# First sums and diagonal copies of a fused attention and MLP kernel in another order, and four low parts of W_o on GpSimd

## The chip, the core and the metric

The kernel runs on one core of a Trainium2 chip. The metric is the device time of one execution in microseconds (us), taken as the median of a few executions; lower is better. The engines are TensorE (PE in the profile, PEld its weight loads), VectorE (DVE), ScalarE (ACT), GpSimd (POOL) and SyncE (SP), whose queue issues most of the DMAs. Each works through its own queue in order and waits on semaphores.

## What is computed

The input x is 2 batches of 2048 tokens with 512 features. Four residual blocks follow each other; the change touches the first, and some small preparations of the others that are made beside it:

```python
def modulated_linear(x, s, aff_w, aff_b, w, b):
    style = s @ aff_w.T + aff_b
    w_mod = w[None] * style[:, None, :]
    demod = rsqrt(sum(w_mod * w_mod, axis=2) + 1e-8)
    return einsum('bni,boi->bno', x, w_mod * demod[:, :, None]) + b

kx = modulated_linear(x, s, k_aff_w, k_aff_b, k_w, k_b).reshape(B, N, 16, 32)
A = softmax(einsum('bnhd,bnjd->bnhj', kx, kx) / sqrt(32), axis=-1)
y = modulated_linear(einsum('bnhj,bnjd->bnhd', A, kx), s, o_aff_w, o_aff_b, o_w, o_b)
x = x + y
x = x + low_rank_layer(x)
x = x + modulated_layer_2(x)
x = x + mlp_of_six_normalized_blocks(x)
```

The attention is among the 16 heads of one token. The MLPs of the last block also have a first layer, SiLU, a second layer and a layer norm of three small state vectors; these are made early on.

## The kernel before

**Tiles.** The 4096 tokens are 32 tiles of 128. `run_order` (L156) has every engine go through the same list of steps: for s from -1 on, `attend(s)` and then `prepare(s)`. In `attend(s)` several tiles are in work at once: `has(o)` means that tile s - o exists. x of tile s + 1 is scaled by the style (GpSimd, L1861), copied to a high part (ScalarE, `xh`, L1138) and its low part subtracted (VectorE, `xl`, L1477); k of tile s is three groups of four products on TensorE (L694: high weight with xh, low weight with xh, high weight with xl), scaled (`kb`, L1450), biased (GpSimd, L1878) and turned (`kt`, L1470); scores, softmax and attention of tile s - 2 use block-diagonal copies that ScalarE makes with four copies each (`diagonal`, L1094: `k_diag` for the scores, `at_diag` for the mix); the mix of tile s - 3 (L666) is turned (`om`, L1426), styled (GpSimd, L1868) and turned back; from step 8 on the output product of W_o (L632) follows. Preparations of weights stand in `prepare(s)` and, on VectorE, in `between(s - 1)` of steps 4 to 7 (L1512).

**Order of the queues in a step.** VectorE: mx and low of tile s - 2, om of tile s - 3, total and rinv of tile s - 2, the low part of o, kb, at, `between`, kt, xl of tile s + 1. ScalarE: high part of o, v and e of tile s - 2, k_diag of tile s - 1, xh of tile s + 1, at_diag of tile s - 2. GpSimd: x of tile s + 1, om of tile s - 3, e times rinv of tile s - 2, bias of kb of tile s. SyncE: x of tile s + 2 once xl of tile s is made (L487); in `prepare(0)` W_o (1 MB), the table rows and three MLP weights (1 MB each, L510 to 513).

**The head.** Ahead of step -1 TensorE runs `keep_busy(ps_o, 5)` (L647), matrix products on a tile of ones that nobody reads, then the style sums (L89); in `prepare(-1)` two more, the row sum of the squares of W_k (L653), the first three products of k of tile 0 (L795) and the column sum, from which VectorE makes the variance (L1533) and GpSimd a power (L1884). VectorE turns that into diagonals, TensorE (L801, L809) and ScalarE (`bc`, L1176) into the factors by which kb is scaled. `styles_turned`, `row_sum`, `column_sum` and `split_low` are the helpers. The waits that matter here:

```python
pe.wait_ge(wsplit_lo[0], C)                       # L793, ahead of the first products of k
dve.wait_ge(wk_in[C - 1], 16)                     # L1388, square 3 of W_k
for c in {3: (), 4: (0,), 5: (1,), 6: (2, 3)}[s]: # L1523, low parts of W_o
    split_low(1, c)
act.wait_ge(wsplit_lo[g], C)                      # L1103, oh of tiles 4 to 7 takes W_o's room
```

Low parts of a weight are `w_raw` minus its high copy (`split_low`, L1380), made where the high parts are ready (`wsplit_hi`; W_o's by ScalarE in `prepare(2)`).

## Time and profile before

| | |
|---|---|
| median of 3 executions | 995.06 us (993.44 to 996.03) |
| the profiled execution, its own time | 994.71 us |
| span of the profile | 992.9 us |
| TensorE busy | 969.8 us, 98% |
| VectorE, ScalarE, GpSimd busy | 664.8, 501.5, 698.5 us |
| mean granted clock of TensorE | 0.991 of full |

The profile is of one execution; times are from the start of the span. Steps -1 to 7 take the first 85 us or so, all 32 tiles of the attention about 330 us, the rest goes to the later blocks. A busy TensorE is not TensorE at its peak, and what another engine waits costs nothing by itself.

### The profile page before, as it was taken

How to read it: one execution, taken by the hardware profiler on the slowest of the kernel's cores; microseconds unless marked ns; L12 is line 12 of the kernel's file. 1: busy time of each engine (PE TensorE's matmuls, PEld its weight loads, DVE VectorE, ACT ScalarE, POOL GpSimd, SP SyncE). 2: the span in 40 equal slices, each digit the busy share in tenths (PEclk: the TensorE clock that was granted, in tenths of full speed). 3: DMA queues.
4: the chain of work that ended last, by engine and by line, in shares of the span. 5: the costliest groups of instructions: out<-in, count | busy, mean ns of one | idle time of the engine just before them, and what ended most of it. 6: DMA issues, size and time to landing. Idle time of an engine off the chain costs nothing.

```text
span 992.9 us, 18147 instructions
## 1 busy us (share of the span) xinstructions
PE 969.8 (98%) x6539; PEld 774.3 (78%) x6539; DVE 664.8 (67%) x1215; ACT 501.5 (51%) x791; POOL 698.5 (70%) x634
## 2 busy tenths in 40 slices
PE   8999999999999999999999999999999999999995
PEld 5567777777777678888888888888888888888884
DVE  6798767689878778666566667657557557565542
ACT  3789878787887555333333343433334334323332
POOL 5557666676675559887777778778768768777861
PEclk7999999999999999999999999999999999999998
DMA  9654654564423562342243143332332233232220
GB/s 279 222 161 139 236 198 151 175 214 147 148 80 95 183 223 75 104 148 95 67 122 120 67 130 103 117 110 80 114 111 72 83 105 121 67 100 100 80 78 22
DMA packets 58557, 125.11 MB, mean 126 GB/s; under 512 B 8051, under 2 KB 12533, under 8 KB 57444
## 3 DMA queue, kind: packets, MB, share of 16 engines
q1 hardware_dynamic: 46692, 82.00, 24.6%
q0 software_dynamic: 11776, 41.95, 13.6%
q8 instruction: 53, 0.87, 0.4%
q14 instruction: 36, 0.29, 0.1%
HBM read 105.98 MB, written 17.95 MB: 125 GB/s over the span
## 4 chain that ended last, share of the span: by engine, by line
PE 75%; POOL 9%; issue 6%; DVE 5%; DMA 2%; ACT 2%; SPq 0%; POOLq 0%; DVEq 0%; ACTq 0%
PE ps L625 37%; PE ps_k L694 7%; PE ps_y L632 7%; PE ps_o L632 6%; PE tp L637 5%; PE ps_v L666 2%; PE ps_s L711 2%; PE ps_u L743 1%; PE tp L972 1%; PE ps_t L756 1%; PE ps_z L960 1%; PE ps_vt L704 1%; DMA path_rows<-in_path,pid 1%; POOL h L1938 1%; POOL om L1868 1%
## 5 line engine op out<-in xcount | busy, mean ns | idle before, releaser
L1924 POOL TENSOR_TENSOR rstd<-var_eps,half 128x1 f32<-128x1 f32 x95 | 54.6, 574 | 95.6 <-DVE var_eps L1672 94.9
L1281 ACT ACTIVATE g_out<-ps 128x512 f32<-128x512 f32 x31 | 18.5, 597 | 163.4 <-PE ps L1077 163.4
L1678 DVE TENSOR_SCALAR shift_n<-mean_var,rstd 128x1 f32<-128x1 f32 x96 | 20.5, 214 | 97.2 <-POOL rstd L1924 95.1
L1868 POOL TENSOR_TENSOR om<-om,bc 128x512 f32<-128x512 f32 x32 | 41.4, 1295 | 62.1 <-DVE om L1426 61.9
L1094 ACT ACTIVATE at_diag<-at 32x512 f32<-32x512 f32 x128 | 80.3, 628 | 7.3 <-DVE at L1458 5.8
L1855 POOL TENSOR_SCALAR xb<-xb,bias_o 128x512 f32<-128x512 f32 x32 | 54.8, 1713 | 40.9 <-DMA xb<-in_x_wide 40.8
L1094 ACT ACTIVATE k_diag<-kt 32x512 f32<-32x512 f32 x128 | 80.1, 626 | 1.1
L1232 ACT ACTIVATE h<-h,shift_n,rstd 128x512 f32<-128x512 f32 x32 | 26.1, 816 | 82.8 <-DVE shift_n L1678 82.8
L1658 DVE TENSOR_TENSOR t_lo<-tp,t_hi 128x512 fp32r<-128x512 f32 x64 | 43.8, 684 | 28.9 <-ACT t_hi L1228 28.9
L1986 POOL DMA_INDIRECT path_rows<-in_path,pid x32 | 41.9, 1309 | 19.5 <-POOL pid L1974 19.5
L694 PE MATMUL ps_k<-wk_hi,xh 128*128 128x512 f32 x128 | 54.7, 430 | 0.7 <-DVE xl L1477 0.7
L625 PE MATMUL ps<-wx_high,x_hi 128*128 128x512 f32 x128 | 53.1, 415 | 0.8 <-DVE x_lo L1720 0.8
L625 PE MATMUL ps<-wt_high,t_hi 128*128 128x512 f32 x128 | 52.8, 412 | 0.0
L1957 POOL TENSOR_TENSOR o<-f,x3s 128x512 f32<-128x512 f32 x31 | 52.5, 1694 | 0.2
L694 PE MATMUL ps_k<-wk_hi,xl 128*128 128x512 f32 x128 | 50.5, 400 | 0.0
L694 PE MATMUL ps_k<-wk_lo,xh 128*128 128x512 f32 x128 | 50.5, 399 | 0.0
L625 PE MATMUL ps<-wx_high,x_lo 128*128 128x512 f32 x128 | 50.4, 394 | 0.0
L1946 POOL TENSOR_TENSOR tt<-xn,comp_rows 128x512 f32<-128x512 f32 x32 | 50.3, 1571 | 0.0
L625 PE MATMUL ps<-wt_high,t_lo 128*128 128x512 f32 x128 | 50.2, 392 | 0.0
L625 PE MATMUL ps<-wt_low,t_hi 128*128 128x512 f32 x128 | 50.0, 390 | 0.0
L625 PE MATMUL ps<-wx_low,x_hi 128*128 128x512 f32 x128 | 49.9, 390 | 0.0
L625 PE MATMUL ps<-ws_high,s_hi 128*128 128x512 f32 x128 | 49.8, 389 | 0.0
(334 smaller groups left out, 3188.8 us busy)
## 6 DMA issues: line engine op xcount, KB each, us to landing
raw<-in_dec_w SPq DMA_DIRECT2D x30, 512.0 KB, 5.4
x_in<-in_x_turned SPq DMA_DIRECT2D x32, 256.0 KB, 5.1
xb<-in_x_wide SPq DMA_DIRECT2D x32, 256.0 KB, 4.3
x_dram<-xb SPq DMA_DIRECT2D x32, 256.0 KB, 3.9
xt<-x_dram SPq DMA_DIRECT2D x8, 1024.0 KB, 8.4
out<-o SPq DMA_DIRECT2D x31, 256.0 KB, 2.1
raw<-in_int_W SPq DMA_DIRECT2D x7, 1024.0 KB, 6.1
id_rows<-in_id_rows SPq DMA_DIRECT2D x32, 64.0 KB
```

The source lines that it names most:

```text
L625: mm = nc.tensor.matmul(out_ps[:, :], x[:, c, :], w_[:, c, :], start=first and n == 0, stop=last and n == len(terms) - 1)
L632: mm = nc.tensor.matmul(out_ps, w_[:, c, at_], x[:, c], start=n == 0, stop=n == len(terms) - 1)
L637: mm = nc.tensor.transpose(bank[:, c, :], src[:, c * P:(c + 1) * P], ident[:, :])
L694: mm = nc.tensor.matmul(ps_k[:, :], x[:, c, :], w_[:, c, :], start=first and n == 0, stop=last and n == len(some) - 1)
L1094: last = nc.scalar.activation(dst[g, :, q, :], src[g, :, :], ACT.Copy)
L1658: nc.vector.tensor_tensor(lo[n][:, :, :], bank[:, :, :], hi[n][:, :, :].bitcast(F32), ALU.subtract).then_inc(lo_ready[n], 1)
L1855: nc.gpsimd.tensor_scalar(xb[n % 3][:, :], xb[n % 3][:, :], bias_o[:, fo:fo + 1], None, ALU.add).then_inc(xb_ready, 1)
L1868: nc.gpsimd.tensor_tensor(om[:, :], om[:, :], bc[:, STYLE_O, t // TB, :], ALU.mult).then_inc(mix_step, 1)
L1924: nc.gpsimd.tensor_tensor(rstd[:, k:k + 1], var_eps[:, k:k + 1], half[:, :], ALU.pow).then_inc(norm_step[k], 1)
L1946: nc.gpsimd.tensor_tensor(tt[:, :], xn[:, :], comp[:, F:2 * F], ALU.mult).then_inc(t_ready, 1)
L1957: nc.gpsimd.tensor_tensor(o[:, :], f2[:, :], x3s[f % 4][:, :], ALU.add).then_inc(o_ready, 1)
L1986: nc.gpsimd.indirect_dma_start(dst[:, :], None, I[table], bass.IndirectOffsetOnAxis(pid[:, k:k + 1], 0)).then_inc(landed, 16)
```

## The change

Seven things, all in steps -1 to 6:
- TensorE's fillers: 6 in place of 5 first, 3 in place of 2 in `prepare(-1)`; the first products of k wait for the high parts of W_k only.
- VectorE's order at the head: low part 0, square 2, style, square 3, low parts 1 and 2. GpSimd squares 0 and 1 only, and makes low part 3 after the first scaling of x.
- VectorE makes the variance of W_k ahead of the two mask copies.
- VectorE makes xl of tile 2 in step 1 ahead of kt of tile 1 (in the other steps the order stays).
- ScalarE: a one-column SiLU on a tile of its own (`first_silu`) and the diagonal copies of k of tile 0 come between the first `bc` copy and the SiLU of the MLPs in `prepare(0)`; they were in `attend(1)`.
- ScalarE: Exp of the block weights in `prepare(1)` in place of `prepare(0)`.
- The four low parts of W_o by GpSimd in steps 4 (part 0), 5 (1 and 2) and 6 (3), in `attend` between the scaling of x and that of om, in place of VectorE in `between`.

```diff
@@ -222,6 +222,7 @@
     aff_kbt, stsq_ko, vareps_ko, half_ko = A["aff_kbt"], A["stsq_ko"], A["vareps_ko"], A["half_ko"]
+    first_silu = A["first_silu"]
     aw, aw_max, aw_low, aw_exp, aw_sum, aw_inv = (A[n] for n in ("aw", "aw_max", "aw_low", "aw_exp", "aw_sum", "aw_inv"))
@@ -644,7 +645,7 @@
             pe.wait_ge(ones_ready, 1)
-            keep_busy(ps_o, 5)
+            keep_busy(ps_o, 6)
             pe.wait_ge(style_k_in, 16 * 3)
@@ -786,11 +787,11 @@
                 if s == -1:
-                    keep_busy(ps_o, 2)
+                    keep_busy(ps_o, 3)
                     pe.wait_ge(style_step, 3)
...
                     row_sum(w_sq[0]).then_inc(squares_step, 1)
-                    pe.wait_ge(wsplit_lo[0], C)
+                    pe.wait_ge(wsplit_hi[0], C)
                     pe.wait_ge(xh_ready, 1)
@@ -1094,6 +1095,14 @@
 
+            def diagonal_key(t):
+                act.wait_ge(k_step, nth(KEYS, "turned", t + 1))
+                if later(t, 2):
+                    act.wait_ge(scores_done, t - 1)
+                else:
+                    act.wait_ge(diag_zero, 3)
+                diagonal(k_diag[t % 2], kt[t % 2]).then_inc(k_diag_ready, 1)
+
             def high_o(t):
@@ -1122,14 +1131,8 @@
                         nc.scalar.activation(ps_s[:, :, :], mask_rows[:, :].unsqueeze(1).to_broadcast((P, PR, D)), ACT.Copy).then_inc(mask_ready, 1)
-                if has(1):
-                    t, p = s - 1, (s + 1) % 2
-                    act.wait_ge(k_step, nth(KEYS, "turned", t + 1))
-                    if later(t, 2):
-                        act.wait_ge(scores_done, t - 1)
-                    else:
-                        act.wait_ge(diag_zero, 3)
-                    diagonal(k_diag[p], kt[p]).then_inc(k_diag_ready, 1)
+                if has(1) and s > 1:
+                    diagonal_key(s - 1)
                 if has(-1):
@@ -1167,6 +1170,8 @@
                     nc.scalar.activation(row_sums[:, :], ps_x[:, :], ACT.Copy).then_inc(style_step, 1)
+                    act.wait_ge(aw_step, 2)
+                    nc.scalar.activation(aw_exp[:, :], aw_low[:, :], ACT.Exp).then_inc(aw_step, 1)
                 if s == 4:
@@ -1175,10 +1180,11 @@
                         if b == 0:
+                            act.wait_ge(demod_bc_ready, 1)
+                            nc.scalar.activation(first_silu[:, :], bc[:, DEMOD_K, 0, 0:1], ACT.Silu)
+                            diagonal_key(0)
                             act.wait_ge(mlp_step, 2)
                             nc.scalar.activation(mlp_h1[0:MLP_ROWS, :], mlp_h1[0:MLP_ROWS, :], ACT.Silu).then_inc(mlp_step, 1)
-                    act.wait_ge(aw_step, 2)
-                    nc.scalar.activation(aw_exp[:, :], aw_low[:, :], ACT.Exp).then_inc(aw_step, 1)
                 if s == 2:
@@ -1382,13 +1388,20 @@
 
+            def square_k(c):
+                dve.wait_ge(wk_in[c], 16)
+                nc.vector.tensor_tensor(w_sq[0][:, c, :], w_raw[0][:, c, :], w_raw[0][:, c, :], ALU.mult).then_inc(square_ready[0], 1)
+
             split_low(0, 0)
+            square_k(2)
+            style_of(0, ps_first, 1)
+            square_k(3)
             split_low(0, 1)
-            style_of(0, ps_first, 1)
-            dve.wait_ge(wk_in[C - 1], 16)
-            nc.vector.tensor_tensor(w_sq[0][:, C - 1, :], w_raw[0][:, C - 1, :], w_raw[0][:, C - 1, :], ALU.mult).then_inc(square_ready[0], 1)
             split_low(0, 2)
-            split_low(0, 3)
+
+            def x_low(t):
+                dve.wait_ge(xh_ready, t + 1)
+                nc.vector.tensor_tensor(xl[:, :, :], x_in[t % 2][:, :, :], xh[:, :, :].bitcast(F32), ALU.subtract).then_inc(xl_ready, 1)
 
@@ -1463,6 +1476,8 @@
                     lift(0)
+                if s == 1:
+                    x_low(s + 1)
                 if has(0):
@@ -1471,10 +1486,8 @@
                     x1_end(s)
-                if has(-1):
-                    t = s + 1
-                    dve.wait_ge(xh_ready, t + 1)
-                    nc.vector.tensor_tensor(xl[:, :, :], x_in[t % 2][:, :, :], xh[:, :, :].bitcast(F32), ALU.subtract).then_inc(xl_ready, 1)
+                if has(-1) and s != 1:
+                    x_low(s + 1)
                 if s == T + 2:
@@ -1520,17 +1533,15 @@
                     nc.vector.tensor_tensor(mlp_h2[m, :], mlp_h2[m, :], vec_be[m, :], ALU.add).then_inc(mlp_step, 1)
-                for c in {3: (), 4: (0,), 5: (1,), 6: (2, 3)}[s]:
-                    split_low(1, c)
 
...
                 if s == -1:
+                    dve.wait_ge(squares_step, 3)
+                    nc.vector.tensor_scalar(vareps_ko[:, 0, :, :], ps_first, 1e-8, None, ALU.add).then_inc(squares_step, 1)
                     dve.wait_ge(consts_in, 16 * 4)
...
                     nc.vector.tensor_copy(mask_rr[0:2, :], e[0:2, :, :].rearrange("p a b -> p (a b)")).then_inc(mask_ready, 1)
-                    dve.wait_ge(squares_step, 3)
-                    nc.vector.tensor_scalar(vareps_ko[:, 0, :, :], ps_first, 1e-8, None, ALU.add).then_inc(squares_step, 1)
                     for b in range(B):
@@ -1843,7 +1854,7 @@
             nc.gpsimd.memset(at_diag[:, :, :, :], 0.0).then_inc(diag_zero, 1)
-            for c in range(C - 1):
+            for c in range(2):
                 pool.wait_ge(wk_in[c], 16)
@@ -1860,6 +1871,11 @@
                                             style_t[:, 0, :, t // TB].unsqueeze(2).to_broadcast((P, C, P)), ALU.mult).then_inc(xm_ready, 1)
+                if 4 <= s < 7:
+                    for c in ((0,), (1, 2), (3,))[s - 4]:
+                        pool.wait_ge(wsplit_hi[1], c + 1)
+                        nc.gpsimd.tensor_tensor(wo_lo[:, c, :], w_raw[1][:, c, :], wo_hi[:, c, :].bitcast(F32),
+                                                ALU.subtract).then_inc(wsplit_lo[1], 1)
                 if has(3):
@@ -1879,6 +1895,9 @@
                 if s == -1:
+                    pool.wait_ge(wsplit_hi[0], C)
+                    nc.gpsimd.tensor_tensor(wk_lo[:, C - 1, :], w_raw[0][:, C - 1, :], wk_hi[:, C - 1, :].bitcast(F32),
+                                            ALU.subtract).then_inc(wsplit_lo[0], 1)
                     pool.wait_ge(squares_step, 4)
@@ -2044,6 +2063,7 @@
             A["xh"] = sb1("xh", [P, C, P], F32R)
+            A["first_silu"] = sb1("first_silu", [P, 1], F32)
             A["xl"] = sb1("xl", [P, C, P], F32R)
```

## Rows read from the trace of the kernel before

**Rows 1.** The page: granted clock of TensorE in 40 slices, tenths of full speed.

```profile
PEclk7999999999999999999999999999999999999998
```

**Rows 2.** Windows: busy us (instructions) of each engine in a stretch, TensorE clock, DMA.

```profile
9.00:10.00 1.00, 0.00 (x0) 0.00 (x0) 0.96 (x3) 0.49 (x1) 1.00 (x1) 0.80 1.03 274
...
19.00:20.00 1.00, 1.00 (x4) 0.81 (x3) 0.91 (x4) 0.00 (x0) 0.24 (x1) 0.58 1.06 371
```

**Rows 3.** Windows of steps 3 to 8, the same columns.

```profile
50.00:60.00 10.00, 7.61 (x122) 5.95 (x119) 8.96 (x16) 9.22 (x16) 5.93 (x8) 1.00 0.59 174
...
70.00:77.00 7.00, 5.43 (x60) 4.35 (x61) 6.71 (x12) 6.23 (x11) 3.63 (x4) 1.00 0.33 115
77.00:90.00 13.00, 13.00 (x153) 9.35 (x154) 11.40 (x21) 11.44 (x20) 11.69 (x9) 1.00 0.73 231
```

**Rows 4.** Chain of waits, 60 to 110 us: start us, us, engine and line.

```profile
76.30 0.64 ACT at_diag L1094
...
76.98 1.08 PE ps_v L666 x32
```

**Rows 5.** Timeline of TensorE, 0 to 45 us: start us, us, what, idle time before it.

```profile
1.18 4.63 PE L644 MATMUL ps_o<-v_t 128*128 128x256 f32 x10 [1.18 <-DVE v_t L1363]
...
7.63 1.11 PE L644 MATMUL ps_o<-v_t 128*128 128x256 f32 x4
10.83 1.94 PE L653 MATMUL ps_x<-wk_sq,sq_wide 128*32 128x512 f32 x8 [2.10 <-DVE wk_sq L1389]
```

**Rows 6.** Timeline of GpSimd, 0 to 45 us.

```profile
35.38 1.05 POOL L1861 TENSOR_TENSOR x_in<-x_in,style_t 128x512 f32<-128x512 f32 x1 [2.86 <-DMA x_in<-in_x_turned]
37.12 1.05 POOL L1872 TENSOR_TENSOR e<-e,rinv 128x512 f32<-128x512 f32 x1 [0.70 <-DVE rinv L1439]
```

**Rows 7.** Timeline of SyncE's queue: DMA issues.

```profile
19.64 2.21 SPq L513 DMA_DIRECT2D raw<-in_res_W  x1
25.25 8.18 SPq L487 DMA_DIRECT2D x_in<-in_x_turned  x2
```

**Rows 8.** DMA issues, 0 to 50 us: size, us from issue to landing.

```profile
raw<-in_res_W SPq DMA_DIRECT2D x1, 1024.0 KB, 15.0
```

**Rows 9.** Tile wk_raw: its readers, duration ns min/median/max, first and last start.

```profile
L1382 DVE TENSOR_TENSOR wk_lo<-wk_raw,wk_hi x4: 677/971/1524, 6.7 to 12.1; 128x512 fp32r<-128x512 f32 x4
L1848 POOL TENSOR_TENSOR wk_sq<-wk_raw x3: 1040/1041/1487, 6.1 to 8.6; 128x512 f32<-128x512 f32 x3
```

**Rows 10.** Timeline of ScalarE, steps 1 and 6.

```profile
28.78 2.53 ACT L1094 ACTIVATE k_diag<-kt 32x512 f32<-32x512 f32 x4
31.34 0.63 ACT L1138 ACTIVATE xh<-x_in 128x512 fp32r<-128x512 f32 x1
...
70.64 0.63 ACT L1121 ACTIVATE e<-low 128x512 f32<-128x512 f32 x1 [0.79 <-DVE low L1419]
...
74.38 2.55 ACT L1094 ACTIVATE at_diag<-at 32x512 f32<-32x512 f32 x4
```

**Rows 11.** Timeline of VectorE, step 2.

```profile
39.44 0.71 DVE L1470 STREAM_TRANSPOSE kt<-kb 128x512 f32<-128x512 f32 x1 [0.53 <-POOL kb L1878]
```

**Rows 12.** Timeline of VectorE, steps 5 and 6.

```profile
67.11 0.68 DVE L1382 TENSOR_TENSOR wo_lo<-wo_raw,wo_hi 128x512 fp32r<-128x512 f32 x1
...
68.34 0.90 DVE L1477 TENSOR_TENSOR xl<-x_in,xh 128x512 fp32r<-128x512 f32 x1
...
74.27 1.33 DVE L1382 TENSOR_TENSOR wo_lo<-wo_raw,wo_hi 128x512 fp32r<-128x512 f32 x1
```

**Rows 13.** Timeline of GpSimd, steps 4 to 6: om of tiles 1 to 3.

```profile
53.98 1.29 POOL L1868 TENSOR_TENSOR om<-om,bc 128x512 f32<-128x512 f32 x1 [2.81 <-DVE om L1426]
...
63.10 1.29 POOL L1868 TENSOR_TENSOR om<-om,bc 128x512 f32<-128x512 f32 x1 [3.77 <-DVE om L1426]
...
71.31 1.29 POOL L1868 TENSOR_TENSOR om<-om,bc 128x512 f32<-128x512 f32 x1 [2.62 <-DVE om L1426]
```

**Rows 14.** Windows, 34 to 36 us, columns as in rows 2.

```profile
34.00:36.00 2.00, 2.00 (x11) 1.63 (x10) 1.34 (x3) 0.59 (x2) 0.62 (x1) 1.00 0.53 143
```

## The prediction

> **What bounds the kernel now.** I read the page first: its clock row shows TensorE at full clock in all slices but the first and the last [rows 1], and TensorE is the engine that is busy nearly throughout. So only two things can shorten this kernel: idle TensorE time, or a slow TensorE clock. The change touches steps -1 to 6 alone, which lie before about 85 us.
>
> The windows show where there is anything to win. In 9 to 10 us the mean clock is 0.80, in 19 to 20 us 0.58 [rows 2]: TensorE ran at half clock, 1.2 instead of 2.4 GHz, from 9.6 to 19.8 us. Later it idles 10 - 7.61 = 2.39 us between 50 and 60 and 7 - 5.43 = 1.57 us between 70 and 77; from 77 on it idles no more [rows 3]. The chain of waits agrees: its last link that is not TensorE is ScalarE's at_diag of tile 4, to 76.94; TensorE's mix of step 7 begins at 76.98 and the chain stays there [rows 4]. The question is thus a narrow one: **how much earlier does at_diag of tile 4 end?** What the change wins upstream and doesn't bring to that point is lost.
>
> The fall of the clock has a visible history. The first fillers run from 1.18 for 4.63 us, the styles follow, two more fillers start at 7.63 and take 1.11, and TensorE then stands still for 2.10 us, until the last square of W_k is there for the row sum at 10.83 [rows 5].
>
> **The wait that caps the head.** GpSimd scales the x tiles in order. Tile 3 is scaled at 35.38, after a wait of 2.86 us for its DMA; behind it in GpSimd's queue stand e of tile 0 (37.12, after 0.70 us for rinv) and the bias add of tile 2 [rows 6]. SyncE issues that DMA at 25.25, so it took 10.1 us; the last MLP weight (res_W), 1 MB, is issued at 19.64 [rows 7] and takes 15.0 us, to 34.6 [rows 8]. The loads land in the order of issue, out of a backlog. After the change x can be issued from 19.64 + 2.21 = 21.85 on, when SyncE's queue is through with that weight; it still lies behind it. I take 35.4 as fixed.
>
> **The change, part by part.**
>
> *Fillers.* One more in the first group is two passes of 4.63/10 = 0.46 us, so the styles start up to 0.9 us later. One more in the second is 2 x 0.28 = 0.55 us [rows 5]; the fillers end near 9.7.
>
> *Squares and low parts of W_k.* VectorE makes squares 2 and 3, GpSimd 0 and 1. GpSimd's third square (up to 1.49 us) leaves the queue ahead of the first x multiply [rows 9], whose start is then set by the style sums. The row sum starts near 10.5, the idle time before it falls from 2.10 to about 0.8 us, and I expect the clock to stay up. The 9.0 us from 10.83 to 19.84 at half clock then shrink by up to 4.5. Low part 3 goes to GpSimd (1.04 to 1.49 us [rows 9]), into a stretch where GpSimd waited for the variance: nothing, and 1.5 us of the head's slack if that cover is gone.
>
> *Products on the high parts alone, variance ahead of the mask copies, xl of tile 2 ahead of kt of tile 1.* These take waits for other work out of queues; their worth is within the head's gain.
>
> *ScalarE.* The Silu table is loaded ahead, and the diagonal copies of tile 0 no longer stand behind Silu, the second broadcast and Exp. They ran from 28.78 for 2.53 us, with xh of tile 2 right behind at 31.34 [rows 10]. Made earlier, they give xh up to 2.5 us, at either clock. Exp and its table load move into step 1, ahead of v and e of tile 0, which wait for TensorE and VectorE: nothing.
>
> *Sum of the head.* The clock (up to 4.5 us) or ScalarE's order (up to 2.5) is each enough to have rinv of tile 0 ready before 36.4. Then e of tile 0 starts when the x multiply ends, 35.38 + 1.05 = 36.4 instead of 37.12 [rows 6], and no earlier. **Term: -0.70 us**, between 0 (no gain in the head) and -0.74 (the gap closed to nothing). VectorE's kt of tile 2 waits for GpSimd's add at 39.44 [rows 11], and moves with it; from there on VectorE and GpSimd work in a closed row of waits, and all follows 0.7 earlier. What TensorE and ScalarE have ready beyond that turns into their idle time.
>
> *W_o's low parts off VectorE.* They are made in steps 5, 6 and 7. Only the one at 67.11 (0.68 us) lies before at_diag of tile 4: it delays kt of tile 5, the xl behind it at 68.34 [rows 12], and so e of tile 4 at 70.64, from which ScalarE works without a pause until at_diag (74.38 + 2.55) is done [rows 10]. That of 74.27 and the two after it come too late: after 77 us TensorE is the bound. So at most -0.68 us. But xl, started earlier, meets more of GpSimd's multiply of the next x tile: it took 0.90 us beside it, where the same subtract takes 0.68 alone and up to 1.52 at the head [rows 9, 12]. I take a gain of 0.3 us.
>
> *W_o's low parts on GpSimd.* Four subtracts of 1.04 to 1.49 us [rows 9], one in step 4, two in 5, one in 6, all between the x multiply and the om multiply, where GpSimd waits 2.81, 3.77 and 2.62 us [rows 13]; they take about 1.2, 2.4 and 1.2. Nothing is late by itself. The high parts are made in step 2, so their wait holds nobody up; if the cover went, e and the bias add behind them would be late by the whole 4.8 us. What they can do is hold up VectorE's xl, which falls into these gaps. An overlap cost 0.22 us (0.90 - 0.68) at 68.34, 0.65 (1.33 - 0.68) at 74.27 [rows 12] and at worst 0.84 at the head. I take 0.1 us in all, since they queue behind a multiply that xl has to pass anyway, with ends 0 and 3 x 0.84 = 2.5. **Term of both: -0.2 us**, between -0.68 and 2.5 - 0.3 = +2.2.
>
> **Sum:** -0.70 - 0.2 = -0.9 us. The profiled execution took 994.71 us (span 992.9), so 993.8; the median shown, 995.06, is 0.35 above it, and against that the forecast is 994.2. The three executions lie 2.6 us apart, so a median may be off by some 0.8. A measurement of this kernel can tell about 0.3%, 3 us, from no change.
>
> **Rivals.**
>
> *A, x of tile 3 lands earlier.* If its landing moves with its issue (3.4 us), or the head's gain passes in another way, the saving is 3.4 to 4.5 us instead of 0.70. For it: the DMA engines carry only 0.53 of their load in 34 to 36 us, just as it lands [rows 14]. Against it: 15.0 and 10.1 us to landing, one behind the other [rows 7, 8]. Time 995.06 - 4.5 - 0.2 = 990.4. Chance 0.12.
>
> *B, the slower end: GpSimd's subtracts hold VectorE.* In steps 4, 5 and 6 one xl on the chain waits each for a whole subtract (1.04 us) that got in first: 3.1 us, against the gains of 0.70 and 0.3. Time 995.06 + 2.1 = 997.2. It turns slower where xl waits over (0.70 + 0.3)/3 = 0.33 us in each step. Against it: the one xl shown beside GpSimd lost 0.22 us. Chance 0.10.
>
> The Trainium skill (SBUF — State Buffer, "SBUF: two separate sides") has a rule for this: a VectorE instruction with two SBUF inputs and a GpSimd instruction take one pair of ports by an exclusive lock, for the whole instruction. By that rule each meeting costs up to the other's whole duration, as in B. The 1.52 against 0.68 us of rows 9 fits it; the xl of rows 12 shows only a part of it.
>
> *C, nothing arrives.* The clock falls all the same, the fillers delay the styles, the copies of tile 0 gain too little, and rinv of tile 0 stays at 37 us: about 995.0. Chance 0.08.
>
> *D, TensorE cools later.* Some 3 us ahead, it idles more between 33 and 41 us. If the clock fell there, steps 3 and 4 would pay about 3 us over their slack: 997.2. Against it: it idled 2.39 us in 50 to 60 and 1.57 in 70 to 77 with the clock at 1.00 [rows 3]. Chance 0.05.
>
> **How the numbers follow.** The forecast holds 0.65; its own range is 993.3 to 995.4. The range for 8 in 10 takes in C, the lower half of B's cost and a part of the way to A: 991.6 to 996.4. Faster by over 0.3% (under 992.1) needs A: 0.13 with the scatter. Slower by over 0.3% (over 998.0) needs the far end of B or D: 0.04. Within it: 0.83.
>
> **What the profile of the changed kernel would show.** The clock at 1.00 from about 6 us on; rinv of tile 0 near 32 us; GpSimd waiting some 8 us for x and scaling tile 3 at 35.4 as before, with e of tile 0 right behind it at 36.4; kt of tile 2 at 38.7; the four subtracts in GpSimd's waits; the mix of step 7 near 76.1. The forecast is wrong if tile 3 is scaled before 35, if the mix of step 7 starts before 75.5 or after 77, or if TensorE idles after 77.

## The result, and the profile after

In ten executions of each kernel the changed one took 998.06 us (996.69 to 999.25) and the one before 995.28 us (993.44 to 997.01): a ratio of 1.0027, interval 1.0019 to 1.0035. It is slower by some 2.7 us where 994.2 was forecast, and lies above the whole range (991.6 to 996.4). The profiled execution took 996.86 us, 2.15 more than that of before.

Three edits that the prediction priced at nothing or with the wrong sign made it slower: one by placing a tile, beyond doubt, the two others by what the profiles show. In the profile the head did what was forecast, but how much of that is the change's own is not shown. First the head, as windows of the changed kernel, which answer to [rows 2, 3]:

```profile
9.00:10.00 1.00, 0.00 (x1) 0.03 (x2) 0.97 (x4) 0.00 (x0) 0.80 (x1) 1.00 1.06 303
19.00:20.00 1.00, 1.00 (x3) 0.14 (x3) 0.00 (x0) 0.66 (x2) 0.48 (x1) 1.00 1.10 379
50.00:60.00 10.00, 7.39 (x130) 5.79 (x121) 8.87 (x16) 9.19 (x16) 8.19 (x7) 1.00 0.51 145
77.00:90.00 13.00, 13.00 (x146) 9.24 (x139) 9.48 (x19) 11.57 (x21) 10.13 (x9) 1.00 0.78 231
```

The clock is at 1.00 (2.4 GHz) where it was 0.80 and 0.58. TensorE's timeline at the head answers to [rows 5]:

```profile
1.18 4.37 PE L645 MATMUL ps_o<-v_t 128*128 128x256 f32 x12 [1.18 <-DVE v_t L1369]
...
7.19 1.54 PE L645 MATMUL ps_o<-v_t 128*128 128x256 f32 x6
10.00 1.07 PE L654 MATMUL ps_x<-wk_sq,sq_wide 128*32 128x512 f32 x8 [1.26 <-DVE wk_sq L1393]
```

TensorE stands still for 1.26 us ahead of the row sum instead of 2.10, and the sum takes 1.07 instead of 1.94. One execution doesn't show that the change keeps the clock up. Two of the kernels below say otherwise: a_end has the program of the changed kernel, fillers included, and b_all32 that of the kernel before, with all large tiles moved alike. Their row sums, a_end first:

```profile
11.09 1.66 PE L654 MATMUL ps_x<-wk_sq,sq_wide 128*32 128x512 f32 x8 [2.30 <-DVE wk_sq L1393]
```

```profile
10.87 1.94 PE L653 MATMUL ps_x<-wk_sq,sq_wide 128*32 128x512 f32 x8
```

a_end waits 2.30 us and its clock is at 0.50 from 11.4 to 21.7 us; b_all32 doesn't wait and stays at 1.00. Over all profiles but b_pe, which never left the lower level, such a fall of 10 us comes in 1 of the 8 with the two more filler rounds and in 7 of the 11 without, each time behind a wait of 1.50 to 2.30 us. Two more (b_vec and a_64_vlow, waits of 1.05 and 1.79) have one of 3.4 us; the rest wait 0 to 1.28 and have none up to 22 us. So the change may make the fall rarer; it doesn't rule it out. GpSimd's timeline, which answers to [rows 6], shows the cap of the head where it was:

```profile
35.28 1.04 POOL L1872 TENSOR_TENSOR x_in<-x_in,style_t 128x512 f32<-128x512 f32 x1 [4.61 <-DMA x_in<-in_x_turned]
36.28 1.05 POOL L1888 TENSOR_TENSOR e<-e,rinv 128x512 f32<-128x512 f32 x1
```

Now the mixes of steps 5 and 7 on TensorE and the k product between them (before, the mixes began at 60.04 and, in [rows 4], at 76.98):

```profile
59.12 1.08 PE L667 MATMUL ps_v<-at_diag,v 128*32 128x128 f32 x32 [1.86 <-ACT at_diag L1095]
60.70 0.50 PE L695 MATMUL ps_k<-wk_hi,xh 128*128 128x512 f32 x1 [0.50 <-DVE xl L1404]
...
76.56 1.08 PE L667 MATMUL ps_v<-at_diag,v 128*32 128x128 f32 x32 [1.55 <-ACT at_diag L1095]
```

The lead is 60.04 - 59.12 = 0.92 us at step 5, and 76.98 - 76.56 = 0.42 us at step 7. So up to 77 us the changed kernel is ahead. But the same mixes in b_all32, with none of the seven edits, are 1.13 and 1.14 us ahead, with x of tile 3 scaled at 35.08:

```profile
58.91 1.08 PE L666 MATMUL ps_v<-at_diag,v 128*32 128x128 f32 x32 [1.86 <-ACT at_diag L1094]
...
75.84 1.08 PE L666 MATMUL ps_v<-at_diag,v 128*32 128x128 f32 x32 [1.58 <-ACT at_diag L1094]
```

So such a lead comes with the old order too, in an execution whose clock doesn't fall at the head. I then set the start of every TensorE instruction against the same one of before. The lead of 0.4 us at 88 us wears off little by little: level at about 135, 0.3 late at 187, 0.9 at 300, 1.42 late from 355 on (some 0.2 of it in one step at 351). At 412 us it jumps by 0.8 us, and 2.2 us stay to the end. A slow drift over 270 us, after the last edited instruction, doesn't look like one late wait; rather, each product takes a little longer. The groups of TensorE by shape, 95 to 330 us (columns: count | busy us, mean ns | idle before), first before, then after:

```profile
L632 PE MATMUL ps_o<-oh,wo_hi 128*128 128x512 f32 x98 | 38.4, 391 | 0.0
L632 PE MATMUL ps_o<-ol,wo_hi 128*128 128x512 f32 x97 | 37.8, 390 | 0.0
L632 PE MATMUL ps_o<-oh,wo_lo 128*128 128x512 f32 x97 | 37.7, 389 | 0.0
L694 PE MATMUL ps_k<-wk_lo,xh 128*128 128x512 f32 x92 | 36.1, 393 | 0.0
```

```profile
L633 PE MATMUL ps_o<-oh,wo_lo 128*128 128x512 f32 x96 | 38.0, 396 | 0.0
L633 PE MATMUL ps_o<-ol,wo_hi 128*128 128x512 f32 x96 | 38.0, 396 | 0.0
L633 PE MATMUL ps_o<-oh,wo_hi 128*128 128x512 f32 x96 | 37.9, 395 | 0.0
L695 PE MATMUL ps_k<-wk_lo,xh 128*128 128x512 f32 x92 | 36.5, 396 | 0.0
```

The code of these products is the same. They overlap, so the mean says less than the distance of two starts: the twelve products of W_o for a tile go from first to last in 2.499 us before (0.227 each) and in 2.570 after (0.234). 32 tiles x 12 x 0.0065 = 2.5 us. That is more than the 1.8 us by which the profile drifts; where the rest is made up the profile doesn't tell.

What differs is where the operands lie. `first_silu` is one column of four bytes and is allotted between `xh` and `xl`. In the built programs it takes 32 bytes per partition, and `xl` and all that is allotted behind it (kb, kt, v, e, at, the diagonal copies, `oh`, `ol`, the room of the squares) start 32 bytes later, while `xh` and the weights `wk` and `wo` stay. TensorE loads a slice of wo while it streams `oh` or `ol`; their distance was a multiple of 512 bytes and is no longer. In the k products a slice of x is loaded and wk is streamed. The group shown at 393 and 396 ns has both its tiles in place; the next slice loaded beside it is one of xl, which moved. Where xl stays (b_o32 below) the group takes 391.

### The profile page after: what moved, and what is told of

Its sections match the earlier page's. It is cut to its first block, busy times and chain, and to the rows that moved or that the text cites. A ratio compares the mean times of both kernels' runs of the same rounds, so it can differ in the third digit from the quotient of the medians.

```text
span 995.1 us, 18156 instructions
## 1 busy us (share of the span) xinstructions
PE 969.0 (97%) x6543; PEld 771.6 (78%) x6543; DVE 664.3 (67%) x1211; ACT 501.0 (50%) x792; POOL 706.7 (71%) x638
## 4 chain that ended last, share of the span: by engine, by line
PE 75%; POOL 8%; issue 6%; DVE 4%; DMA 3%; ACT 1%; SPq 1%; POOLq 0%; DVEq 0%; ACTq 0%
PE ps L626 37%; PE ps_k L695 7%; PE ps_y L633 7%; PE ps_o L633 6%; PE tp L638 5%; PE ps_s L712 2%; PE ps_v L667 2%; PE ps_u L744 1%; DMA x_in<-in_x_turned 1%; PE ps_t L757 1%; PE ps_vt L705 1%; PE tp L973 1%; PE ps_z L961 1%; DMA path_rows<-in_path,pid 1%; POOL h L1957 1%
## 5 line engine op out<-in xcount | busy, mean ns | idle before, releaser
L1976 POOL TENSOR_TENSOR o<-f,x3s 128x512 f32<-128x512 f32 x31 | 50.4, 1625 | 0.2
L626 PE MATMUL ps<-ws_low,s_hi 128*128 128x512 f32 x128 | 49.8, 389 | 0.0
```

Source lines behind the costliest of these rows:

```text
L626: mm = nc.tensor.matmul(out_ps[:, :], x[:, c, :], w_[:, c, :], start=first and n == 0, stop=last and n == len(terms) - 1)
L1976: nc.gpsimd.tensor_tensor(o[:, :], f2[:, :], x3s[f % 4][:, :], ALU.add).then_inc(o_ready, 1)
```

## The experiments

All ratios are to the kernel before on the same chip, over five rounds except where one execution is said. The medians in us are of several chips; it is the ratios that compare.

**The gap alone.** Into the kernel before, behind `xh`, an unused tile:

```diff
             A["xh"] = sb1("xh", [P, C, P], F32R)
+            sb1("gap", [P, 1], F32)       # b_gap64: [P, 16]
```

> The kernel before, with an unused tile of one column between xh and xl and nothing else: all tiles from xl on (kt, k_diag, the o tiles oh and ol, xb) start 32 bytes later, at 32 modulo 64 bytes instead of 0. Theory P (place): TensorE reads a tile that starts there more slowly. In the profile of the changed kernel the W_o products of 95 to 330 us take 395 to 396 ns where they took 389 to 391, and the step from one to the next is 0.234 instead of 0.227 us: 12 products in each of 32 tiles, 0.007 us each, is 2.7 us, and some 0.5 us more for the k products: 998.3 against 995.3, ratio 1.003. Rival Q (work): the loss comes from the order or from GpSimd's subtracts; then this kernel is at 995.3, ratio 1.000.

> The kernel before, with an unused tile of 16 columns (64 bytes) in the same place: the same tiles move by 64 bytes and stay at 0 modulo 64. Theory P: 995.3, ratio 1.000, and W_o products at 389 to 391 ns. If any move of these tiles costs time (another theory of the place, for instance which tiles share a region), this is at about 998 as well. Rival Q: 995.3.

b_gap32: 996.93 us, ratio 1.0034 (1.0021 to 1.0047). b_gap64: 995.75, 1.0016 (1.0006 to 1.0025). Nothing computes with the tile, and 32 bytes cost about as much as the whole change does net (the intervals overlap). The groups of b_gap32 are those of after:

```profile
L632 PE MATMUL ps_o<-oh,wo_lo 128*128 128x512 f32 x96 | 38.0, 396 | 0.0
L632 PE MATMUL ps_o<-ol,wo_hi 128*128 128x512 f32 x96 | 38.0, 396 | 0.0
L632 PE MATMUL ps_o<-oh,wo_hi 128*128 128x512 f32 x96 | 37.9, 395 | 0.0
```

With 64 bytes a block of twelve takes 2.534 us, half of the way, and so does the time. So the expectation of 1.000 for b_gap64 missed: it isn't the start modulo 64 that decides.

**Start or distance.** The same gap ahead of all large tiles (every start moves by 32 bytes, every distance stays), and ahead of `oh`, `ol` and `xb` alone, each one execution:

```diff
+        sb("gap", [P, 1], F32)            # b_all32, ahead of u_parts
         u_parts = sb("u_parts", [P, B, C, P], F32R)
...
+            sb1("gap", [P, 1], F32)       # b_o32
             A["oh"], A["ol"] = [], []
```

> The kernel before, with an unused tile of one column ahead of all large tiles: weights, x, k and o tiles all start 32 bytes later, at 32 modulo 64, with the same distances between them. If the distance between the tile that is streamed (oh, ol) and the weights that are loaded beside it decides, the W_o products stay at 0.227 us from one to the next (12 in 2.50 us, first to last). If the start by itself decides, they take 0.234 as in b_gap32 (2.57).

> The kernel before, with an unused tile of one column ahead of oh, ol and xb alone: xl, kt, k_diag, at_diag and the rest stay. If the W_o products carry the loss, they take 2.57 us from first to last of 12 as in b_gap32, the k products stay as before, and the run is about 2.5 us slower than before. If the loss comes from the k tiles, this run is as before.

b_all32 took 994.47 us, b_o32 996.12. Their groups, b_all32 first:

```profile
L632 PE MATMUL ps_o<-oh,wo_hi 128*128 128x512 f32 x98 | 38.4, 392 | 0.0
L632 PE MATMUL ps_o<-oh,wo_lo 128*128 128x512 f32 x98 | 38.1, 389 | 0.0
```

```profile
L632 PE MATMUL ps_o<-oh,wo_hi 128*128 128x512 f32 x96 | 38.2, 397 | 0.0
L632 PE MATMUL ps_o<-oh,wo_lo 128*128 128x512 f32 x96 | 37.9, 394 | 0.0
```

The blocks of twelve take 2.500 and 2.573 us. By these blocks a start at 32 costs nothing; the distance between `oh` or `ol` and the weights does. In b_o32, TensorE's lag grows from 0.14 us at 90 us to 1.9 at 362.

**The change at other places.** `first_silu` with 16 columns (a_64), the same with W_o's low parts back on VectorE (a_64_vlow), and `first_silu` allotted behind the last tile, so that no tile moves (a_end):

```diff
-            A["first_silu"] = sb1("first_silu", [P, 1], F32)
+            A["first_silu"] = sb1("first_silu", [P, 16], F32)[:, 0:1]   # a_64
...
             A["xb"] = [sb1(f"xb{i}", [P, WIDE]) for i in range(3)]
+            A["first_silu"] = sb1("first_silu", [P, 1], F32)            # a_end
```

> The changed kernel, whole, but first_silu has 16 columns, so that all tiles behind it start at 0 modulo 64 again. Theory P: the head's gain of about 0.4 us is all that is left, so 994.9, ratio 0.9996; the W_o products are back at 389 to 391 ns. Rival Q: 998.0, ratio 1.0027, as the change itself.

> As a_64, but W_o's four low parts are made by VectorE in steps 5 to 7 as before, none by GpSimd. By the prediction's sum the other parts of the change bring 0.70 us, and this part 0.2: 994.6 to 995.0, and at most 0.5 us from a_64. By rival B of the prediction (GpSimd's subtracts hold VectorE) it is up to 3 us faster than a_64; the mix of step 7 then starts well before 76.5 us.

> The changed kernel, whole, but first_silu is allotted behind xb, so that no other tile moves. Theory P (place of xl and the tiles behind it): W_o products at 0.227 us each as before, and what is left is the order's gain, some 0.4 us: ratio 0.9996 to a kernel before, and some 3 us faster than the change (ratio 1.0027). Rival Q (the order or GpSimd's subtracts cost the time): ratio 1.0027 as the change.

a_64: 997.41, 1.0033 (1.0021 to 1.0045), no better than the change itself, though its blocks of twelve are back half of the way as b_gap64's are; 0.9996 was expected, and why it is no better is not known. a_64_vlow: 995.84, 1.0020 (1.0010 to 1.0029). a_end: 996.15, 1.0012 (1.0003 to 1.0021); its blocks take 2.499 us again. 0.9996 was expected here too. So the placement explains the larger part (1.0027 against 1.0012, on two chips), and about 1 us is still there that the forecast doesn't know.

**W_o's low parts on GpSimd.** Taken out of the unshifted change (a_end_vlow), and put alone into the kernel before (b_plow):

```diff
+                if 4 <= s < 7:                         # b_plow, GpSimd behind the scaling of x
+                    for c in ((0,), (1, 2), (3,))[s - 4]:
...
-                for c in {3: (), 4: (0,), 5: (1,), 6: (2, 3)}[s]:   # b_plow, VectorE
-                    split_low(1, c)
```

> The change with first_silu allotted last (no tile moves) and W_o's four low parts back on VectorE in steps 4 to 6. The run with first_silu last alone was 1.0012 [1.0003, 1.0021]. Theory H (GpSimd's pair of subtracts in step 5, 3.42 us at 58.37, holds up VectorE's xl; TensorE idles 1.86 and 0.50 us there and its clock then falls for 3.4 us): without them no fall near 60, mix of step 7 at 75.9 to 76.3, and the time 0.7 to 1.2 us under the run with first_silu last: ratio 0.9995 to 1.0005. Rival G (the cost sits at 397 to 412 us, where in every kernel of the change so far, with GpSimd's low parts or without, GpSimd waits 1.5 to 1.6 us for the gathered path rows where the kernel before and its padded copies wait 0.7 to 0.8): that wait stays at 1.5 to 1.6, the step of +0.8 us in TensorE's lag at 412 us stays, and the ratio is 1.001 or more. Both can hold: then the lag is about -0.9 at 90 us and 0.0 at the end, ratio 1.000.

> The kernel before with only W_o's four low parts moved to GpSimd in steps 4 to 6, behind the scaling of x; nothing else, no tile added. Theory H: xl of step 5 is held up beside GpSimd's pair, TensorE idles some 1.5 us more around 57 to 61 us, the clock may fall there for 3.4 us; mix of step 7 at 77 to 78 instead of 76.3, ratio 1.0008 to 1.0015. Rival (the pair hides, as the prediction had it with +0.1 for contention and -0.3 for VectorE): mix of step 7 at 76.0 to 76.4 and ratio 0.9995 to 1.0003. For the wait on the gathered path rows near 398 us: if GpSimd's own longer program makes it, it is 1.5 to 1.6 us here too, and TensorE's lag steps up by 0.8 us at 412; if another part of the change makes it (the Silu ahead, the moved orders of VectorE), it stays at 0.7.

a_end_vlow: 995.48, 1.0004 (0.9995 to 1.0013). b_plow: 995.95, 1.0011 (1.0000 to 1.0021). No interval settles it alone, but all three pairs (a_64 and a_64_vlow too) point to a cost of 0.8 to 1.3 us, and the timeline shows 0.5 of it. Step 5 in b_plow, GpSimd, VectorE, TensorE:

```profile
57.73 1.22 POOL L1859 TENSOR_TENSOR x_in<-x_in,style_t 128x512 f32<-128x512 f32 x1
58.91 3.43 POOL L1864 TENSOR_TENSOR wo_lo<-wo_raw,wo_hi 128x512 fp32r<-128x512 f32 x2
```

```profile
60.05 1.14 DVE L1477 TENSOR_TENSOR xl<-x_in,xh 128x512 fp32r<-128x512 f32 x1
```

```profile
59.66 1.08 PE L666 MATMUL ps_v<-at_diag,v 128*32 128x128 f32 x32 [1.87 <-ACT at_diag L1094]
61.24 0.50 PE L694 MATMUL ps_k<-wk_hi,xh 128*128 128x512 f32 x1 [0.50 <-DVE xl L1477]
```

GpSimd's pair lies over xl, which takes 1.14 us; in the kernel before and in a_end_vlow the same subtract took 0.64. TensorE waits the missing 0.50 us for it, in this kernel and in after, a_end and a_end_dma, and in none that leaves the low parts on VectorE. (In a_64 xl takes 1.14 us as well, but the mix beside it runs at half clock and covers it.) From the mix of step 5 to that of step 7 it is 76.98 - 60.04 = 16.94 us before and 77.10 - 59.66 = 17.44 in b_plow: +0.50, and no trace of a gain on VectorE. (The 76.3 that the expectations compare with is the last part of at_diag, [rows 4]; the mix itself begins at 76.98.) The other half of what the expectation of a_end_vlow named fell: the clock drops to 0.50 for 3.4 us near 60 us in a_end, a_64 and a_end_dma, but also in b_dma and a_end_vlow_dma, which have no such subtracts, and not in after or b_plow. Where it does, the way from the mix of step 5 to that of step 7 takes 18.4 us or more in place of 16.9. It comes and goes with the execution: in 3 of 5 profiles with the subtracts and in 2 of 14 without. Whether they make it likelier is open, and with it where the rest of the 0.8 to 1.3 us lies.

**The MLP weights behind x.** SyncE issues the second and third MLP weight in `prepare(1)`, in the unshifted change (a_end_dma), also without GpSimd's low parts (a_end_vlow_dma), and in the kernel before (b_dma):

```diff
-                    for j, n in enumerate(MLPS):
-                        sp.dma_start(mlp_w2[j][:, :, :], ...)
+                    sp.dma_start(mlp_w2[0][:, :, :], ...)
+                if s == 1:
+                    for j, n in enumerate(MLPS[1:], 1):
+                        sp.dma_start(mlp_w2[j][:, :, :], ...)
```

> As a_end, and SyncE issues the second and third MLP weight (1 MB each) in prepare(1), behind x of tile 3, in place of prepare(0). By the prediction's cap (x of tile 3 lies behind that backlog, GpSimd waits for it till 35.3 us) x now lands near 29, e of tile 0 starts at about 33.7 (when its rinv is there) in place of 36.3, and the mix of step 7 comes about 2 us earlier: ratio 0.9975. If the cap isn't what holds the head, the ratio is that of a_end.

> The change with first_silu last, W_o's low parts on VectorE, and SyncE issuing the second and third MLP weights one step later, behind x tile 3. Theory H: the head's gain (x tile 3 scaled near 30.7 instead of 35.3; mix of step 7 near 75.0) and no fall near 60: 1.2 us under the run with first_silu last and W_o's parts on VectorE, and 0.5 to 1.0 us under the run with only the DMAs moved (0.9993): ratio 0.9983 to 0.9990. Rival G: the wait on the gathered rows stays at 1.6 us and TensorE gives 0.9 us of its lead back at 404 to 412: ratio 0.999 at best, no better than the run with the DMAs moved by more than 0.3 us.

> The kernel before with one edit only: SyncE issues the second and third MLP weights one step later, behind x tile 3. If the head is capped by the landing of x tile 3 (scaled at 35.4 before, 30.7 with the two weights moved), the mix of step 7 comes 0.3 to 1.1 us earlier; here the rest of the head (rinv of tile 0 at 33 us, kt of tile 2) may become the cap, which the change's new order moves ahead and the kernel before doesn't. With neither the shifted tiles, nor GpSimd's low parts, nor the later gather: ratio 0.9985 to 0.9995, and the wait on gathered path rows 0.7. If DMA isn't the cap without the change's order: mix of step 7 within 0.2 of 76.3 and ratio 0.9998 to 1.0003.

a_end_dma: 994.46, 0.9993 (0.9983 to 1.0003). a_end_vlow_dma: 994.79, 0.9989 (0.9977 to 1.0001). b_dma: 994.56, 0.9996 (0.9986 to 1.0005). GpSimd at the head of a_end_dma:

```profile
30.73 1.04 POOL L1874 TENSOR_TENSOR x_in<-x_in,style_t 128x512 f32<-128x512 f32 x1
33.86 1.05 POOL L1890 TENSOR_TENSOR e<-e,rinv 128x512 f32<-128x512 f32 x1 [2.09 <-DVE rinv L1454]
```

In this profile x tile 3 is no longer the cap. It is scaled 4.55 us earlier than in after, rinv of tile 0 ends last, e starts 2.4 us earlier and the mix of step 7 at 75.50. The ratio expected was 0.9975. In b_dma, x is early too (32.37), but e starts at 37.03, behind 3.17 us of waiting for rinv. The clock was at 0.50 from 9.9 to 20.2 us there; b_all32 has rinv 1.8 us earlier (34.90) with the old order and the clock up, so it isn't shown that the change's order is needed. Its mix of step 7, expected by 76.5 at the latest, began at 78.48, behind the fall near 60 us. The profile of a_end_vlow_dma missed as well: x tile 3 was scaled at 35.66 for 30.7, e started at 38.80 behind 2.09 us for rinv, the clock was at 0.50 from 24.5 to 31.3 us, and the mix of step 7 began at 80.09. It was the longest of its twelve executions, 999.09 us. None of the three is beyond doubt faster than the kernel before; a_end_dma and a_end_vlow_dma are the lowest and clearly beat the changed kernel.

**The jump at 412 us.** It is there in every version of the change, and each engine's part alone tells whose it is: TensorE's two filler rounds (b_pe, b_pe5), ScalarE's part (b_act, b_act5), the orders of VectorE and GpSimd without W_o's low parts (b_vec, b_vec5), all without a shift. b_pe, b_act and b_vec are one execution each.

```diff
-            keep_busy(ps_o, 5)                        # b_pe
+            keep_busy(ps_o, 6)
...
-                    keep_busy(ps_o, 2)
+                    keep_busy(ps_o, 3)
```

> The kernel before with the change's two more filler rounds on TensorE alone (6 for 5, 3 for 2), no other edit. What is tested: whether the wait on gathered path rows near 398 us (0.7 before, 1.5 to 1.6 in every version of the change) and the small transfer on an instruction queue 1 us behind the issue of that gather follow from the place of instructions in TensorE's program. If so: wait 1.5 to 1.6, that transfer early, TensorE's lag steps up by 0.8 us at 412. If another engine's program does it: wait 0.7.

> The kernel before with the change's ScalarE part alone (the first Silu on one column, its tile allotted last, the first diagonal copy and the Exp moved ahead), no other edit. If ScalarE's program sets the place of the early transfer on an instruction queue: the wait on gathered path rows is 1.5 to 1.6 us and TensorE's lag steps up by 0.8 at 412; otherwise 0.7. The head: the diagonal copy of tile 0 no longer behind the Silu, x tile 3 still scaled at 35.3 to 36: mix of step 7 within 0.3 of 76.3.

> The kernel before with the change's orders on VectorE and GpSimd alone (squares 2 and 3 on VectorE ahead, the last low part of W_k on GpSimd, TensorE's first k products waiting for the high parts, x's low part of step 1 ahead, the sum of the squares ahead), no other edit, W_o's low parts left on VectorE. If VectorE's or GpSimd's program sets the place of the early transfer: the wait on gathered path rows is 1.5 to 1.6 us, otherwise 0.7. If none of the three parts does it alone, it is the sum of them. Mix of step 7 within 0.5 of 76.3.

> The kernel before with the change's ScalarE part alone, again, now timed against the kernel before (the single look gave 993.50 us, granted clock 0.998 with no stretch at the low level, mix of step 7 1.1 us early, 0.8 us early at the end). If the ScalarE part is a gain of its own: ratio 0.9985 to 0.9995, and this is a version that beats both kernels. If the single look was a good draw (the kernel before itself gives 993.2 to 993.5 in executions at 0.997 to 0.998): ratio 0.9995 to 1.0005.

> The kernel before with the two more filler rounds alone, again: the first execution ran at the lower level of TensorE's clock over its whole span (0.556, 1621 us) and says nothing of the edit. If fillers alone keep the clock up between 9 and 20 us: no such stretch in the profile and ratio 0.999 to 1.000; if they only delay the first row sums: 1.000 to 1.0005. The wait on gathered path rows: 0.7 if TensorE's program has no part in it (the ScalarE part alone gave 0.6, the VectorE and GpSimd part 1.0), 1.5 if it has.

> The kernel before with the change's orders on VectorE and GpSimd alone, again, now timed (the single look gave 994.57 us, mix of step 7 0.8 us early, a stretch at the low clock at 9 to 14 us, 0.8 us given back at 189 to 193 us and the end level with the kernel before). If this giving back belongs to the kernel: ratio 0.9997 to 1.0005; if it was this execution's: 0.9990 to 0.9997. With the change's three parts so timed, their sum stands against the whole without W_o's low parts and without the shift (1.0004).

b_pe ran at the lower level of the clock over its whole span (mean 0.556, 1623 us) and says nothing of its edit. b_act 993.50, b_vec 994.57. b_act5: 994.22, 0.9998 (0.9989 to 1.0007). b_pe5: 994.57, 1.0006 (0.9995 to 1.0017). b_vec5: 995.25, 1.0007 (0.9997 to 1.0016). None of the three parts alone is told from the kernel before, and b_act's 993.50 was, as its second expectation allowed for, a good draw. GpSimd near 398 us, its issue of the gather of path rows, of the last gather behind it, and the product that needs them, in the kernel before, in after and in b_pe5:

```profile
392.48 2.95 POOL L1986 DMA_INDIRECT path_rows<-in_path,pid  x1 [0.28 <-POOL pid L1974]
...
397.11 1.13 POOL L1986 DMA_INDIRECT scal<-in_scale,pid  x1 [0.30 <-issue]
398.93 1.28 POOL L1938 TENSOR_TENSOR h<-xn,path_rows 128x512 f32<-128x512 f32 x1 [0.69 <-issue]
```

```profile
393.89 2.95 POOL L2005 DMA_INDIRECT path_rows<-in_path,pid  x1 [0.28 <-POOL pid L1993]
...
401.18 1.28 POOL L1957 TENSOR_TENSOR h<-xn,path_rows 128x512 f32<-128x512 f32 x1 [1.53 <-issue]
```

```profile
392.13 2.96 POOL L1986 DMA_INDIRECT path_rows<-in_path,pid  x1 [0.28 <-POOL pid L1974]
...
399.76 1.28 POOL L1938 TENSOR_TENSOR h<-xn,path_rows 128x512 f32<-128x512 f32 x1 [1.87 <-issue]
```

From issue to product it is 6.45 us before, 7.29 after and 7.63 in b_pe5. Further down the chain TensorE waits for it, before and in b_pe5:

```profile
412.48 0.63 PE L637 MATMUL tp<-ident,ss 128*128 128x128 f32 x4 [0.36 <-DVE t_lo L1658]
```

```profile
413.26 0.63 PE L637 MATMUL tp<-ident,ss 128*128 128x128 f32 x4 [1.50 <-DVE t_lo L1658]
```

b_pe5 is 0.34 us ahead of the kernel before until there and 0.78 behind from there on. In this profile two filler rounds in the first 10 us cost 1.1 us at 412. The DMA view has the link: a load of 0.02 MB on an instruction queue. The quarter of a microsecond in which it shows, 398.23 to 398.48 before (5.75 us behind the issue of the gather) and 395.63 to 395.88 in b_pe5 (3.50 behind):

```profile
q8 instruction: 1, 0.02, 24.1%
```

```profile
q0 software_dynamic: 6, 0.02, 101.2%
q8 instruction: 1, 0.02, 43.3%
```

In b_pe5 it falls among the packets of the gather (the software queue). This holds without exception over all 19 profiles that reach there at full clock: 11 without the two rounds have the load 5.5 to 5.75 us behind the issue and a wait of 0.59 to 0.97 us; 8 with them have it at 3.5 to 4.5 and wait 1.5 to 2.15. That the rounds make the wait is shown by b_pe5 and by this split; that it goes through this load is what the rows suggest, not tried by itself. My expectation of another, small load 1 us behind the issue was wrong: it comes with ScalarE's part (b_act, b_act5 have it, with waits of 0.59 and 0.62) and does nothing.

## Why the prediction was wrong, by its own steps

**The head: right in the profile, not shown to be the change's.** Clock at 1.00 throughout, x of tile 3 at 35.28 (35.38 before and forecast), e of tile 0 at 36.28 (36.4), kt of tile 2 at 38.60 (38.7), rinv of tile 0 at 33.44 (near 32). The term of -0.70 came out as -0.92 at step 5. But b_all32 has -1.13 there without the change, and a_end, with it, +0.56, behind the fall of the clock at 11.4 us. The prediction took the fall in one profile for a property of the kernel; it belongs to the execution. Of 117 timed executions of the kernel before, 33 have a mean granted clock of 0.996 or more, and by the medians of each chip they took 0.2 to 1.8 us less than those under 0.994. So part of the term may have been in the median of 995.06 already, and no timed version with the new head and SyncE's order unchanged is faster than the kernel before. Rival A did not occur. The cap was real, as a_end_dma shows. It also scatters: x of tile 3 was scaled between 34.69 and 36.77 us in executions of versions with SyncE's order unchanged, more than the term itself.

**W_o's low parts, wrong in sign.** The step took -0.3 for VectorE and +0.1 for GpSimd. The runs show no gain and +0.50 us at one place, where GpSimd's two subtracts run back to back for 3.42 us over the xl that TensorE needs next. Inside the bounds given, and rival B's mechanism at one step of its three, without its size: mix of step 7 at 76.56 where 76.1 was forecast. The Trainium skill (SBUF — State Buffer, "SBUF: two separate sides") has the shared pair of ports held by one engine for a whole instruction, the other blocked. The rows agree that the two hinder each other (xl 1.14 us for 0.64, wo_lo 1.72 for a single one at 50.11 us in after, 1.28 for the one at 68.83), and that the loss, 0.50, is below a whole instruction.

**The step that failed: `first_silu`.** Under *ScalarE* the prediction has "The Silu table is loaded ahead" and prices the instruction's place in the queue; that its output is a new tile, put in the middle of the list of tiles, was not considered at all. It moved the streamed operands by 32 bytes against the weights and cost 1.8 us in the profile (0.4 ahead at 88 us to 1.42 behind at 355), 3.4 us as timed by itself (b_gap32, 1.0034), some 1.5 as timed between the change and a_end, and alone turns the forecast's sign. Not all of the 1.8 need be its own: between the same two points the profiles of unshifted versions lose -0.1 to 1.2 us, most of them 0.3 to 0.9, in steps near 191 and from 342 to 351 us, and those shifted by 32 bytes lose 1.7 to 1.9. The sentence "from 77 on it idles no more" was true and was taken to mean that nothing can be lost there: idle time isn't the only way in which a bound engine loses. The Trainium skill (SBUF — State Buffer, "SBUF: two separate sides") says that on the engines' side only the port pair of GpSimd and VectorE causes contention and TensorE never waits on anyone. By that rule a shift of 32 bytes costs nothing. The measurement decides: 389 to 391 ns became 395 to 396 by the placement alone, whatever inside TensorE's path makes it.

**Fillers, wrong.** They were costed at a later start of the styles, up to 0.9 us; the styles start at 5.61 us before, 5.39 in after and 6.46 in b_pe5. The long fall at the head is absent in 7 of 8 profiles with them (three of these have a shorter one between 14 and 32 us) and present in a_end. What they cost in the profile, 0.8 us, came 400 us later through the wait for gathered rows.

**The sum by measurement:** -0.92 head, +0.50 low parts, +1.8 placement, +0.8 the jump: +2.2 us, as these two profiles differ (995.1 - 992.9); timed, it is 2.7. Rival C (nothing arrives) is out for the profile of after, where 0.4 us did arrive at 77 us, but a_end's is just that case: the clock falls all the same and the mix of step 7 begins at 79.63. Rival D's fall, behind 33 to 41 us, is in no profile; the one near 60 us is in five, though not in that of after, and 5 of 7 versions of the change show a fall somewhere between 11 and 66 us. What stays open: a_end_vlow, with neither shift nor low parts, measured 1.0004, and its profile is 0.54 us ahead at 88 us, level at 355 and 0.89 behind from 414 on, so beside the jump another 0.5 us goes that no run explains; and some leads shrink by 0.1 to 1.2 us at 189 to 193 us in part of the executions, a few us behind a wait of GpSimd for the DMA of xb (6.7 to 7.9 us before, in after, b_act and b_vec).

## What to carry to other kernels

Put a new tile, even one of four bytes, behind the others, and compare the distances of streamed and loaded operands before and after. When a kernel drifts evenly after the last edited instruction, compare the mean duration of the same products before looking for a wait. Before moving work into an idle stretch of GpSimd, look what VectorE runs on the critical path in that stretch, and don't put two such instructions back to back. Before crediting a gain at the head to a new order, look at an execution of the unchanged kernel with the same clock.

## What the runs showed of the hardware that was not expected

- The same matrix product started every 0.227 us with the streamed tile a multiple of 512 bytes from the weights loaded beside it, every 0.234 us with 32 bytes more, and every 0.230 with 64 more; moving both together changed nothing (0.227).
- Where a program's instructions lie matters far away: four more TensorE instructions at the head moved an instruction load by some 2 us at 396 us, and the product that needs a gather started 7.29 to 7.91 us behind the gather's issue in place of 6.36 to 6.54; that the one makes the other is not tried by itself.
- One execution ran wholly at the lower level of TensorE's clock, 1623 us, with an edit of no weight; the same kernel took 994.57 afterwards. One of b_dma's took 1082.14 us at a mean granted clock of 0.851, with a median of 994.56.
- With the same instructions, the clock at the head fell for 10 us in some executions and not in others; the mean granted clock of the unchanged kernel went from 0.989 to 0.998 over 117 executions.
